# A decoder block on one core: row maxima carried as rows of the score contraction, residual additions on PE, epsilons on ScalarE, and an earlier load of the first weight codes

## The chip, the cores and the metric

The kernel runs on one core of a Trainium2 chip. The metric is the device time in microseconds of one execution, lower is better. The engines are PE (TensorE), DVE (VectorE), ACT (ScalarE), POOL (GpSimd) and SP (SyncE, here only a queue of DMA transfers). PEld is PE's weight load.

## The reference

Input x has 8 batches of 128 tokens and 256 channels. Three blocks follow one another, each on a layer norm of x and added to x:

```python
x = x + attn(layernorm(x), Wq, Wk, Wv, Wo)          # 16 heads of 16, T = 128
x = x + xattn(ctx, ctx, layernorm(x), ssm_kernel, D) # long convolution of k*v products, then times q
x = x + ffn(layernorm(x), gate, up, down)            # 256 -> 2048 -> 256, 4-bit weights with block scales

# attn
scores = einsum('bthd,bshd->bhts', q, k) * tril(ones)   # masked scores are 0, not -inf
out = softmax(scores / T ** 0.5) @ v @ Wo
# xattn, per head of width 8: kv[i,j,l] = k[i,l] * v[j,l]
out = irfft(rfft(kv) * rfft(ssm_kernel)) + kv * D;  out = sum_i out[i,j] * q[i]
# ffn
out = (gelu_tanh(x @ Wg.T) * (x @ Wu.T)) @ Wd.T
```

Since a masked score is 0 and still takes part in the softmax, each row needs the exponential of its negative maximum as well, times the sum of the later values.

## The kernel before

Products that need precision run on PE as three fp16 products of high and low parts (`three`, L927), or in fp32.

Start: x is loaded and normalised, transposed by PE (`transpose_x`), projected to Q and K in two halves of four batches (`project_qk`), with V between and after. Q and K, split in fp16 high and low parts in `nat`, go through a DRAM scratch (L312) and come back packed in `QK` (L322): partitions 0 to 63 hold the even heads, 64 to 127 the odd ones, 64 rows each (high, low and the repeated part). Ten heads of the convolution (`convolve`, L980 to L984) run meanwhile; the other six are spread over the first ticks.

Tick loop: the rest of attention, the second block and the layer norms run as a software pipeline. Every engine walks through the same ticks t, and in each tick through its own hand-written list of steps; `batch(t, T_X)` says which batch a step treats: batch b is treated in tick T_X + 2b. Two ticks pass per batch, the even and the odd one treating half of the heads each. A batch passes, among others:

- tick 0 and 1: `scores(b, p)` on PE into banks 0 and 1, with the causal mask added by products of `identb`/`swapb` with masks (`causal`, L999) and the fp16 contraction of 64 rows (L1016); DVE's `pair_max` (L788) reads the row maxima.
- tick 2, 3: POOL's `guard_max` (L443) copies the maxima with the last row guarded; PE transposes them (L1117), ACT copies them to `mT` (L645) and takes their exponential (L571).
- tick 4, 5: `scores_t` on PE, the transposed scores in banks 2 and 3: masks again (L999), the maxima subtracted by an fp32 product of `sel` with `mT` (L1035), and the contraction (L1039). ACT's `probs` takes the exponential (L579).
- tick 5 to 7: `attend` (L1055), ACT's `pv_out`, token transposes (L1154) and the sum over later values (L1158) on PE, DVE's `normalise`.
- tick 8: transpose of the output (L1133), ACT's copy, projection (L1168), DVE's residual addition (L869) and statistics.
- tick 9, 10: POOL's `rstds` (epsilon L373, power L378, shift L380), ACT's `ln_apply` (L629), query transposes (L1148), ACT's `qx`.
- tick 11 to 15: POOL's `conv_products` (L457, L460), DVE's `sum_slots` (L840), residual and transpose by PE (L1123, L1125), ACT's copy to X (L666), statistics, `rstds`, `ln_apply`, transposes for the FFN (L1141).

Decode: `load_codes(j)` on SP's queue brings step j's codes and scales; `codes_split`, `codes_join` on DVE, `decode_scale` on POOL (L473), `w_hi_step` on ACT (L601) and `w_lo` on DVE (L830) make fp16 high and low weights of them. Steps 0 to 3 do so at the ticks of `DECODE`; steps 0 and 1 use `XN`'s space.

FFN: 32 units, `gate_and_up(u)` (L927, 12 products of 512 columns) and `down(u)` (L1097, 12 of 256 columns). The first eight are placed at `UNIT_TICKS` 22 to 29, the others follow the tick loop. ACT, DVE and POOL each do one operation or two per unit (L618, L608, L848, L481). The order is fixed by the lists and semaphores; nothing is planned at run time. `take(n, sem, count)` makes PE wait for the last reader of bank n.

## Time and profile before

| what | value |
|---|---|
| median of 3 runs | 283.21 us (281.93 to 284.2) |
| profiled execution: its time | 285.32 us |
| profiled execution: its span | 283.6 us |
| mean granted TensorE clock | 0.973 |
| PE busy | 258.4 us (91%) |
| PEld, DVE | 167.5 us (59%), 160.6 us (57%) |
| ACT, POOL | 123.2 us (43%), 157.2 us (55%) |

The span runs from the first to the last instruction of one profiled execution. Busy time of PE is modelled at its ends, so a busy PE need not be at its peak. Busy shares are means over stages that have different limits. A row "start us, us" gives when a group of operations began and how long it took; `x24` is the count.

### The profile page before, as it was taken

To read this page: it belongs to the slowest core of one execution; us is meant where nothing else is said; L and a number is where in the kernel's file an instruction comes from. 1 tells how busy PE (TensorE), PEld (TensorE's weight loads), DVE (VectorE), ACT (ScalarE), POOL (GpSimd) and SP (SyncE) were. 2 spreads that over 40 slices of the span, in tenths; PEclk is the share of its full clock that TensorE was granted. 3 is DMA by queue.
4 is the path that set the end of the run, shared out by engine and by line. 5 is a ranking of instruction groups with operands and counts; after the bars stand their busy time and mean duration, and the time that the engine had idled before them with its cause. 6 is when DMAs were issued, how large, how long until landed. Compare 5 with 4: busy or idle time off the path is not lost.

```text
span 283.6 us, 5339 instructions
## 1 busy us (share of the span) xinstructions
PE 258.4 (91%) x2056; PEld 167.5 (59%) x2056; DVE 160.6 (57%) x264; ACT 123.2 (43%) x257; POOL 157.2 (55%) x193
## 2 busy tenths in 40 slices
PE   0699999997999999996969999999999999999993
PEld 0355766555777777664634566666555666556662
DVE  2879633367775987897576584252635436131124
ACT  2354676553654545644426455323534253442240
POOL 3277264250514788799989897336445563723330
PEclk9999999997999999999579999999999999999998
DMA  6986969707120000003000200000303000000004
GB/s 208 380 296 198 225 203 225 160 4 218 37 82 0 2 2 2 1 3 111 2 0 1 83 30 0 2 0 0 113 0 103 11 0 2 1 0 2 0 0 149
DMA packets 16185, 20.27 MB, mean 71 GB/s; under 512 B 1056, under 2 KB 13856, under 8 KB 16160
## 3 DMA queue, kind: packets, MB, share of 16 engines
q1 hardware_dynamic: 16160, 19.93, 24.4%
q8 instruction: 16, 0.26, 0.4%
q14 instruction: 9, 0.07, 0.1%
HBM read 16.26 MB, written 3.67 MB: 70 GB/s over the span
## 4 chain that ended last, share of the span: by engine, by line
PE 67%; POOL 8%; DMA 7%; DVE 7%; SPq 4%; issue 3%; ACT 2%; DVEq 0%; ACTq 0%; POOLq 0%
PE bank L927 31%; PE bank L1097 14%; PE bank L1035 4%; DMA XN<-in_down_scale 4%; PE bank L999 3%; PE bank L1168 3%; PE bank L1055 3%; POOL w L473 3%; DMA qk_scratch<-pvs 2%; SPq L312 2%; POOL arena L457 2%; POOL arena L460 2%; DMA X<-in_x 1%; DVE arena L741 1%; PE bank L1158 1%
## 5 line engine op out<-in xcount | busy, mean ns | idle before, releaser
L481 POOL TENSOR_TENSOR QK<-QK 128x512 f16<-128x512 f32 x31 | 36.0, 1162 | 56.1 <-ACT QK L608 56.1
L848 DVE SCALAR_TENSOR_TENSOR QK<-bank,QK 128x512 f32<-128x512 f32 x32 | 22.1, 692 | 66.8 <-PE bank L927 66.8
L618 ACT ACTIVATE QK<-bank 128x512 f32<-128x512 f32 x32 | 19.1, 597 | 71.1 <-PE bank L927 71.1
L927 PE MATMUL bank<-xTh,Wa 128*128 128x512 f16 x128 | 40.9, 381 | 0.0
L927 PE MATMUL bank<-xTh,Wb 128*128 128x512 f16 x128 | 40.7, 379 | 0.0
L457 POOL TENSOR_TENSOR arena<-Ys,qx 128x640 f32<-128x640 f32 x16 | 25.1, 1570 | 8.8 <-ACT qx L660 8.8
L579 ACT ACTIVATE PT<-bank 128x1024 f32<-128x1024 f32 x16 | 16.4, 1023 | 27.4 <-PE bank L1039 27.4
L788 DVE TENSOR_REDUCE mx<-bank 128x8 f32<-128x1024 f32 x16 | 19.6, 1222 | 15.1 <-PE bank L1016 15.0
L927 PE MATMUL bank<-xTl,Wa 128*128 128x512 f16 x64 | 24.3, 380 | 0.0
L927 PE MATMUL bank<-xTl,Wb 128*128 128x512 f16 x64 | 24.3, 379 | 0.0
L1097 PE MATMUL bank<-Wa,QK 128*128 128x256 f16 x192 | 23.6, 273 | 0.0
L1097 PE MATMUL bank<-Wb,QK 128*128 128x256 f16 x192 | 23.3, 273 | 0.0
L1035 PE MATMUL bank<-mT,sel 48*128 48x128 f32 x256 | 22.3, 292 | 0.0
L1097 PEld LDWEIGHTS bank<-Wa,QK 128*128 128x128 f16 x192 | 18.7, 98 | 5.7 <-POOL QK L481 0.3
L473 POOL TENSOR_TENSOR w<-arena 128x768 f32<-128x768 f16 x12 | 21.9, 1824 | 0.0
L413 POOL TENSOR_TENSOR arena<-arena 128x320 f32<-128x320 f32 x16 | 14.3, 902 | 13.6 <-PE bank L984 13.6
L1097 PEld LDWEIGHTS bank<-Wb,QK 128*128 128x128 f16 x192 | 18.7, 98 | 5.3
L1035 PEld LDWEIGHTS bank<-mT,sel 48*128 48x128 f32 x256 | 19.6, 190 | 2.6 <-issue 0.3
L927 PEld LDWEIGHTS bank<-xTh,Wa 128*128 128x128 f16 x128 | 12.6, 99 | 13.6 <-issue 0.3
L927 PEld LDWEIGHTS bank<-xTh,Wb 128*128 128x128 f16 x128 | 12.6, 98 | 13.4
L608 ACT ACTIVATE QK<-QK 128x512 f16<-128x512 f32 x32 | 19.9, 621 | 1.0 <-DVE QK L848 1.0
L840 DVE TENSOR_REDUCE R<-arena 128x128 f32<-128x1024 f32 x16 | 19.0, 1209 | 2.1 <-POOL arena L460 2.1
(136 smaller groups left out, 522.1 us busy)
## 6 DMA issues: line engine op xcount, KB each, us to landing
QK<-qk_scratch SPq DMA_DIRECT2D x16, 256.0 KB, 6.0
arena<-in_codes SPq DMA_DIRECT2D x6, 384.0 KB
arena<-in_ker SPq DMA_DIRECT2D x2, 1024.0 KB, 12.5
qk_scratch<-Wa SPq DMA_DIRECT2D x16, 128.0 KB
arena<-in_ctx SPq DMA_DIRECT2D x2, 768.0 KB, 8.1
arena<-in_gu_scale SPq DMA_DIRECT2D x6, 256.0 KB
out<-XN SPq DMA_DIRECT2D x4, 256.0 KB, 2.4
Wb<-in_wqkv SPq DMA_DIRECT2D x3, 256.0 KB, 5.0
```

The lines of the kernel that those rows point to most:

```text
L457: g_.tensor_tensor(view(Z[:, r], [[64, H], [1, NPAIR], [NSLOT, HD]], rows), view(Ys[:, 0, 0], [every, [DIAG, NPAIR], [1, HD]], convolved), ...
L473: g_.tensor_tensor(W32[:, nib, :], view(bits(j).bitcast(F16), [[2, 768]], nib), scales(j), ALU.mult).then_inc(s_w32, 1)
L481: g_.tensor_tensor(il[:, u % IR], val[:, u % VR], ih[:, u % IR], ALU.subtract).then_inc(s_il, 1)
L579: s_.activation(PT[:, 2 * (n % 2):2 * (n % 2) + 2].rearrange("p g h t -> p g (h t)"), psum[:, 2:4, :], ACT.Exp, scale=SCALE).then_inc(s_ex ...
L608: s_.activation(ih[:, u % IR], val[:, u % VR], ACT.Copy).then_inc(s_ih, 1)
L618: s_.activation(val[:, u % VR], bank[2 * (u % 2)][:, :], ACT.Gelu_apprx_tanh, scale=1.0 / W_GAIN).then_inc(s_gel, 1)
L788: v_.tensor_reduce(mx[:, b % 2, 8 * p:8 * p + 8], psum[:, 0:2, :].rearrange("p g (h t) -> p (g h) t", h=4), AX.X, ALU.max).then_inc(s_max, 1)
L840: v_.tensor_reduce(R[:, b % 2, H * half:H * half + H], view(Z[:, b % 2], [[NSLOT, H * HD], [1, NSLOT]], 1024 * half), AX.X, ALU.add).then_ ...
L848: v_.scalar_tensor_tensor(out=val[:, u % VR], in0=bank[2 * (u % 2) + 1][:, :], scalar=UP_SCALE, in1=val[:, u % VR], op0=ALU.mult, op1=ALU. ...
L927: ins = mmul(out, a(c), w(c), start=(n == 0), stop=(n == 3 * len(chunks) - 1))
L1035: mmul(bank[2 + par][:, P * j:P * j + P], view(sel[mrows, 4 * (2 * p + par) + j:4 * (2 * p + par) + j + 1], [[0, P]]), mT[mrows, b % 2, :] ...
L1097: last = mmul(out, a[:, u % IR, t], w[j % RW][:, nib, 512:768], start=((j, nib) == (0, 0) and tt % 2 == 0 and n == 0), stop=((j, nib) == ( ...
```

## The change

- **Row maxima.** `QK` packs 48 rows a half instead of 64 (high, low, and one repeat), and two rows more: on the K side of the transposed pass (`QK[..., 1]`, rows 48 and 49 of each half) the constant -8, on the Q side (`QK[..., 0]`) the row maxima over 8, as an fp16 high and low part. Their product in the contraction subtracts the maximum. DVE makes the parts (`max_pieces`), PE transposes them in fp16, ACT copies them to `mT`, and SP's queue writes them into `QK` by two small DMAs a batch (`max_rows`). The products of `sel` and `mT` go, and so does POOL's `guard_max`.
- **Masks.** `causal` uses two groups of 256 columns a pass instead of one of 512 and one of 256.
- **Residuals.** The first residual, too, is added by an identity product of X into bank 7, and evicted to X by ACT; DVE's addition goes.
- **Epsilons** of the second and third norm are added on ACT (`ln_eps`).
- **Codes.** Step 0's codes are loaded before the second Q/K half goes through the scratch; steps 1 to 3 are issued from ACT's queue.
- **Order.** One convolution head more lies in the ticks; `T_SPLIT`, `T_PROJ`, `T_MIX2` and `T_RT` move by a tick; steps 2 and 3 are decoded at ticks 19 and 23 (before 16 and 22); each engine's list has a new order. PE runs identity products (`keep_busy`) while it waits at the start.

The core of the diff (constants and lists that only swap places are left out):

```diff
-            0, 2, 3, 4, 5, 6, 7, 7, 8, 8, 8, 9, 9, 10, 11, 11, 12, 12, 13, 13, 14, 15, 15)
-        CONV_EARLY = 10
+            0, 1, 3, 4, 5, 6, 7, 7, 8, 9, 8, 9, 9, 10, 11, 12, 12, 12, 13, 13, 14, 15, 15)
+        CONV_EARLY = 9
...
-        DECODE = (1, 5, 16, 22)
+        DECODE = (1, 5, 19, 23)
         DECODE_AHEAD = 7
+        WARM = (18, 4, 6)
...
+            sp.wait_ge(s_const, 3)
             for g in range(2):
-
+                for par in range(2):
+                    sp.dma_start(QK[64 * par + 48:64 * par + 50, g, 1],
+                                 view(minus, [[0, H // 2], [1, HALF]])).then_inc(s_minus, 16)
+            for g in range(2):
+                if g == 1:
+                    load_codes(sp, 0)
...
+                        for part in range(2):
+                            sp.dma_start(scr[g, k, part, :, 8 * m:8 * m + 8],
+                                         nat[g][k][:, m, part, :]).then_inc(s_scr[2 * g + k], 16)
                 for k in range(2):
...
+                        for first, parts, row in ((0, 2, 0), (0, 1, 32)) if k == 0 else ((0, 1, 0), (0, 2, 16)):
...
+            def max_rows(b):
+
+                sp.wait_ge(s_mt, b + 1)
+                for par in range(2):
+                    rows = 64 * par + 48
+                    sp.dma_start(QK[rows:rows + 2, b // 4, 0, :, P * (b % 4):P * (b % 4) + P],
+                                 mT[H * par:H * par + H, b % 2, :]).then_inc(s_rows[b % 2], 16)
+
+            for b in range(B):
+                max_rows(b)
+            for j in range(EARLY, STEPS):
+                load_codes(sp, j)
             for b in range(0, B, 2):
...
-            def guard_max(b):
-
-                r = b % 2
-                pool.wait_ge(s_max, 2 * b + 2)
-                if b >= 2:
-                    pool.wait_ge(s_em, b - 1)
-                    pool.wait_ge(s_mpt, b - 1)
-                g_.tensor_scalar(view(mm[:, r, :], [[64, 2], [1, H]]), view(mx[:, r, :], [[0, 2], [1, H]]),
-                                 guard[:, 0:1], None, ALU.max).then_inc(s_mch, 1)
...
+            def ln_eps(ln, b):
+
+                sc.wait_ge(s_mv[ln], b + 1)
+                s_.activation(veps[:, b:b + 1], mv[:, b, 1:2], ACT.Identity, bias=eps[:, 0:1]).then_inc(s_veps[ln], 1)
...
+                    if j + 1 < EARLY:
+                        load_codes(sc, j + 1)
...
+                for b in batch(t, T_LN2):
+                    sc.wait_ge(s_proj, b + 1)
+                    s_.activation(X[:, b, :], bank[7][:, 0:D], ACT.Copy).then_inc(s_x1, 1)
...
+            def max_pieces(b):
+
+                r = b % 2
+                ve.wait_ge(s_max, 2 * b + 2)
+                if b == 0:
+                    ve.wait_ge(s_const, 7)
+                if b >= 2:
+                    ve.wait_ge(s_em, b - 1)
+                    ve.wait_ge(s_mpt, b - 1)
+                hi = view(mp[:, r], [[16, 2], [4, 2], [1, 4]])
+                lo = view(mp[:, r], [[16, 2], [4, 2], [1, 4]], 8)
+                by_half = [[4, 2], [8, 2], [1, 4]]
+                v_.tensor_scalar(ms[:, r], mx[:, r], guard[:, 0:1], 1.0 / MAX_GAIN, ALU.max, ALU.mult).then_inc(s_ms, 1)
+                v_.tensor_scalar(hi, view(mx[:, r], by_half), guard[:, 0:1], 1.0 / MAX_GAIN,
+                                 ALU.max, ALU.mult).then_inc(s_ms, 1)
+                ve.wait_ge(s_ms, 2 * b + 2)
+                v_.tensor_tensor(lo, view(ms[:, r], by_half), hi, ALU.subtract).then_inc(s_mch, 1)
...
-                    v_.tensor_tensor(X[:, b, :], X[:, b, :], bank[7][:, 0:D], ALU.add).then_inc(s_x1, 1)
...
+            def keep_busy(n):
+
+                for _ in range(n):
+                    mmul(bank[7][:, 0:P], ident[:, :], ident[:, :], start=True, stop=True)
+
...
-            def causal(banks, mask, swapped, full):
+            def causal(banks, transposed):
 
                 half = [slice(0, 64), slice(64, P)]
-                for k in (full, 1 - full):
-                    width = P if k == full else 64
-                    first = 64 if k == 1 and width == 64 else 0
+                for k in range(2):
                     for par in range(2):
                         rows = half[par]
-                        pick, m = (identb, mask) if par == k else (swapb, swapped)
-                        mmul(view(banks[par][:, :], [[P, 4], [1, width]], first), pick[rows, :],
-                             view(m[rows, first:first + width], [[0, 4], [1, width]]),
-                             start=(k == full), stop=False, skip_group_check=True)
+                        if transposed:
+                            pick = (identb if par else swapb) if k == 0 else prevb
+                            m, cut, first = (below, 1, 64) if k == 0 else (below, 0, 0)
+                        else:
+                            pick = (swapb if par else identb) if k == 0 else nextb
+                            m, cut, first = (above, 0, 0) if k == 0 else (above, 1, 64)
+                        mmul(view(banks[par][:, :], [[P, 4], [1, 64]], first), pick[rows, :],
+                             view(m[rows, cut:cut + 64], [[0, 4], [1, 64]]),
+                             start=(k == 0), stop=False, skip_group_check=True)
 
             def scores(b, p):
...
-                        rows = slice(64 * par, 64 * par + 64)
+                        rows = slice(64 * par, 64 * par + 48)
...
                     for par in range(2):
-                        mrows = slice(64 * par, 64 * par + 48)
-                        mmul(bank[2 + par][:, P * j:P * j + P], view(sel[mrows, 4 * (2 * p + par) + j:4 * (2 * p + par) + j + 1], [[0, P]]),
-                             mT[mrows, b % 2, :], start=False, stop=False, skip_group_check=True)
-                    for par in range(2):
-                        rows = slice(64 * par, 64 * par + 64)
+                        rows = slice(64 * par, 64 * par + 50)
...
+                for b in batch(t, T_PROJ):
+                    take(7, s_x1, b + 1)
+                    pe.wait_ge(s_ott, b + 1)
+                    if b == 0:
+                        pe.wait_ge(s_w[3], 16)
+                    mmul(bank[7][:, 0:D], ident[:, :], X[:, b, :], start=True, stop=False)
+                    for c in range(2):
+                        last = mmul(bank[7][:, 0:D], oT[:, b % 2, c, :], wo[:, c, :], start=False, stop=(c == 1))
+                    last.then_inc(s_proj, 1)
```

`load_codes(q, j)` is the same function as before with its queue as an argument. In PE's list of a tick the new order is: projection, plain scores, residual and R transposes, transpose of the maxima, transposed scores, query transposes, FFN transposes, token transposes, output transpose, `attend`, units, convolutions. In ACT's: query copies, `ln_apply` of norm 3, eviction to X of block 2, epsilon of norm 3, output copy, maxima, `probs`, `pv_out`, epsilon of norm 2, units, FFN transposes, decode and its load, `ln_apply` of norm 2, convolutions, eviction to X of block 1.

## Rows read from the trace of the kernel before

**Rows 1.** Windows, all engines: busy us, instructions, granted clock, DMA share, GB/s.

```profile
61.55:72.98 11.43, 9.94 (x153) 7.02 (x154) 7.67 (x9) 4.83 (x6) 2.72 (x4) 0.85 0.48 139
...
81.21:89.66 8.45, 8.45 (x128) 6.32 (x129) 4.96 (x9) 4.13 (x9) 2.19 (x5) 1.00 0.01 2
...
98.10:107.73 9.63, 9.59 (x134) 7.17 (x134) 8.38 (x14) 4.81 (x11) 7.56 (x12) 1.00 0.01 2
107.73:117.19 9.46, 9.12 (x125) 6.95 (x125) 7.12 (x14) 5.09 (x13) 7.54 (x12) 1.00 0.01 2
117.19:126.86 9.67, 8.77 (x112) 6.54 (x111) 9.22 (x16) 5.35 (x12) 9.40 (x9) 1.00 0.01 3
...
137.35:148.46 11.11, 8.31 (x30) 6.47 (x27) 7.80 (x13) 3.61 (x8) 9.48 (x15) 0.65 0.00 0
148.46:277.60 129.14, 128.20 (x787) 77.81 (x786) 55.54 (x75) 49.50 (x84) 69.32 (x61) 1.00 0.06 19
```

**Rows 2.** Chain of work that ended last: start us, us, what.

```profile
12.04 7.26 PE bank L927 x24
...
21.16 0.68 DVE xTl L708
...
46.33 10.01 DMA XN<-in_down_scale
...
268.48 2.59 PE bank L927 x12
271.07 1.31 PE bank L1097 x12
```

**Rows 3.** Timeline of PE, one tick from 81.21: start us, us, what.

```profile
81.21 0.39 PE L999 MATMUL bank<-maskw_t,swapb 64*128 64x512 bf16 x1
...
81.55 0.39 PE L1035 MATMUL bank<-mT,sel 48*128 48x128 f32 x4
...
82.83 0.37 PE L999 MATMUL bank<-maskb,identb 64*128 64x512 bf16 x1
...
83.16 0.39 PE L1016 MATMUL bank<-QK 64*128 64x128 f16 x8
83.47 0.32 PE L1117 MATMUL bank<-ident,mm 128*112 128x128 f32 x1
```

**Rows 4.** Groups by form: count, busy us, mean ns of one, idle before.

```profile
L1123 PE MATMUL bank<-X,ident 128*128 128x256 f32 x16 | 5.3, 418 | 0.0
...
L373 POOL TENSOR_SCALAR veps<-mv 128x1 f32<-128x1 f32 x16 | 4.3, 266 | 8.0 <-DVE mv L697 6.8
...
L869 DVE TENSOR_TENSOR X<-X,bank 128x256 f32<-128x256 f32 x8 | 3.3, 418 | 4.2 <-PE bank L1168 4.2
...
L803 DVE RECIPROCAL rec<-num 128x16 f32<-128x16 f32 x8 | 2.0, 253 | 0.3
...
L571 ACT ACTIVATE em<-mm 128x16 f32<-128x16 f32 x8 | 1.7, 208 | 0.0
```

**Rows 5.** Timeline of POOL, 116 to 139 us.

```profile
116.65 1.56 POOL L457 TENSOR_TENSOR arena<-Ys,qx 128x640 f32<-128x640 f32 x1 [1.38 <-ACT qx L660]
...
124.22 3.77 POOL L473 TENSOR_TENSOR w<-arena 128x768 f32<-128x768 f16 x2
...
138.48 0.27 POOL L380 TENSOR_SCALAR shift<-mv,rstd 128x1 f32<-128x1 f32 x1
```

**Rows 6.** DMA issues: count, KB each, median us to landing.

```profile
QK<-qk_scratch SPq DMA_DIRECT2D x16, 256.0 KB, 6.0
...
out<-XN SPq DMA_DIRECT2D x4, 256.0 KB, 2.4
```

**Rows 7.** Timeline of SP's DMA queue: one load of the codes.

```profile
62.67 0.36 SPq L336 DMA_DIRECT2D XN<-in_codes  x1
63.07 0.61 SPq L338 DMA_DIRECT2D XN<-in_gu_scale  x1
63.73 0.59 SPq L341 DMA_DIRECT2D XN<-in_down_scale  x1
```

More of the change, by code:

```diff
@@ L314, in _ @@
                 for k in range(2):
[L315 removed]
+                    sp.wait_ge(s_scr[2 * g + k], 64)
                     for par in range(2):
[L317 to L323 removed]
@@ L387, in _ @@
                     g_.memset(vaug[:, :, :, DH:DH + 1], 1.0).then_inc(s_const, 1)
-            for m, sign in ((maskb, 1), (mask_t, -1)):
+            half = [slice(0, 64), slice(64, P)]
+            for m, keep, base in ((above, ALU.is_ge, 0), (below, ALU.is_ge, -1)):
+                sign = 1 if m is above else -1
                 own(g_.memset(m[:, :], 0.0))
-                own(g_.affine_select(out=m[:, :], in_=m[:, :], compare_op=ALU.is_ge, fill=NEG, base=0,
-                                     pattern=[[-sign, P]], channel_multiplier=sign))
-            for m, sign in ((maskw, 1), (maskw_t, -1)):
-                own(g_.memset(m[:, :], 0.0))
-                for half, base in ((slice(0, 64), 64), (slice(64, P), 0)):
-                    own(g_.affine_select(out=m[half, :], in_=m[half, :], compare_op=ALU.is_ge, fill=NEG,
-                                         base=sign * base, pattern=[[-sign, P]], channel_multiplier=sign))
+                for rows in half:
+                    own(g_.affine_select(out=m[rows, :], in_=m[rows, :], compare_op=keep, fill=NEG, base=base,
+                                         pattern=[[-sign, 65]], channel_multiplier=sign))
             own(g_.memset(swapb[:, :], 0.0))
@@ L662, in _ @@
                                   ACT.Copy).then_inc(s_qx, 1)
+                for b in batch(t, T_APPLY3):
+                    ln_apply(2, b)
                 for b in batch(t, T_LN3):
@@ L855, in _ @@
                     w_lo(j)
-                for b, p in pair_of_groups(t, T_SCORES):
-                    pair_max(b, p)
+                for b in batch(t, T_SUM2):
+                    sum_slots(b, 1)
+                for h in conv_heads(t + 1):
+                    if h >= KVR:
+                        products(h)
+                for b in batch(t, T_LN2):
+                    ve.wait_ge(s_x1, b + 1)
+                    ln_stats(1, b)
+                for j in early_decode(t, 0):
+                    codes_split(j)
+                    codes_join(j)
+                for b in batch(t, T_SPLIT):
+                    max_pieces(b)
                 for b in batch(t, T_LN3):
@@ L1113, in _ @@
                     scores(b, p)
-                for b in batch(t, T_MPT):
-                    take(7, s_mt, b + 1)
-                    pe.wait_ge(s_mch, b + 1)
-                    t_.transpose(bank[7][0:112, 0:P], mm[:, b % 2, :], ident[:, :]).then_inc(s_mpt, 1)
                 for b in batch(t, T_RT):
@@ L1142, in _ @@
                     last.then_inc(s_yt, 1)
-                for b in batch(t, T_QT):
-                    take(6, s_qx, 2 * b + 2)
-                    pe.wait_ge(s_xn[1], b + 1)
-                    for c in range(2):
-                        last = t_.transpose(bank[6][:, P * c:P * c + P], XN[:, b, P * c:P * c + P], ident[:, :])
-                    last.then_inc(s_qt, 1)
                 for b in batch(t, T_TOK):
```

257 lines of the change are left out of this document (130 added, 127 removed).

## The prediction

> **What bounds the kernel now.** I read the windows first, cut at the places where the attention projection of a batch (L1168) ends or the tick loop enters a new stretch, then the chain of waits, then the order of PE's work inside one tick.
>
> PE is the busy engine nearly everywhere, but for three different reasons. From 148.46 on it is full: 128.20 us busy out of 129.14 [rows 1]. In the chain this is one pattern repeated: 2.59 us of L927, then 1.31 us of L1097, 3.90 us a unit [rows 2]; 32 units are 124.8 us, and the change leaves them alone. So the end is the time at which unit 0 starts, plus about 129 us, plus the 6 us behind it. Between 61.55 and 117.19 PE is busy as well (8.45 of 8.45; 9.59 of 9.63), but with attention work that the change cuts [rows 1]. From 117 to 148 PE has gaps (8.77 of 9.67, then 8.31 of 11.11 at a granted clock of 0.65), while POOL is busy for 9.40 and 9.48 us: POOL sets the pace there, with DVE close to it (9.22) where a decode step falls in [rows 1]. A saving on PE passes through whole in the first stretch only as far as DVE (8.38 of 9.63) lets it, and in the last only if POOL's queue also starts earlier.
>
> **Part 1: row maxima as two rows of the contraction.** One tick's PE order is in [rows 3]. The transposed pass takes 0.34 us of masks (81.21 to 81.55) and 1.28 us of body (81.55 to 82.83), where L1035 adds the maxima in fp32 beside the fp16 products. The plain pass has masks of 0.33 and a body of only 0.31 (83.16 to 83.47). The new transposed body is of that form, 50 rows deep: it saves 0.97 a pass, 1.94 a batch. The masks shrink from 512 + 256 columns to 256 + 256, two thirds: 0.11 for each of four mask groups, 0.44 a batch. The transpose of the maxima shrinks too; I give it 0.1. Against this stands one more identity product per batch for the residual; L1123 is the same product, 5.3 us for eight batches, 0.66 each with modelled ends [rows 4]; I take 0.5. Net 2.0 us a batch, 16 us of PE work.
>
> What is added elsewhere: DVE loses the residual addition (0.42) and gets three operations on 16 or fewer elements a batch; the nearest row is the reciprocal of 16 elements, 0.25 [rows 4]. So DVE goes up by 0.3 a batch. POOL loses its maximum operation and two epsilons (0.27 each, about 0.3 with the gap); ScalarE gets them, nearest row L571 with 0.21 [rows 4], and gets the eviction of X.
>
> The maxima now travel by DMA: ScalarE's copy, two issues on SP, a landing, then PE's transposed pass. The trace has no small transfer on a quiet queue. The nearest rows are 2.4 us for the output and 6.0 for the packed Q/K rows, both 256 KB [rows 6]; an issue costs 0.36 to 0.61 [rows 7]. I take the output's value: 0.3 + 2 x 0.5 + 2.4 = 3.7 us. Behind the transpose PE has, until the pass that needs the rows, a transposed pass (0.55), the attention products and token transposes (about 1.5) and a plain pass (0.55): 2.6 us, 3.0 where the later transposes join. So PE waits about 1 us a batch while PE is the bound, and nothing where DVE or POOL is. Behind that wait on PE lie the query transposes, the attention products and the projection; ScalarE's exponentials wait for it. The Trainium skill, "DMA: Bandwidth & Descriptors" (section "Anatomy of one DMA"), puts the fixed part of a transfer at about 2.0 us; by that the wait would be 0.6, and the sum some 2 us lower over the early batches. No row here shows so small a transfer.
>
> **Part 2: the start.** PE does its first 24 projection products in 7.26 us [rows 2]; 24 at the late rate (2.59 / 12 = 0.216) are 5.2. The added identity products fill the idle start, so that these may run at the higher clock: 2.1 us. But the second projection waits for DVE's split of x, which ends at 21.84 [rows 2] after DVE operations that hang on POOL and on x, not on PE. I pass on 0.8 us (ends 0 and 2). Moving one convolution head behind tick 0 shifts work, and saves none.
>
> **Part 3: the first codes.** The 10.01 us transfer of the first codes stands in the chain [rows 2]; it ends at 56.34, and decode, ScalarE's conversion and DVE's rest follow. The window 61.55 to 72.98 is 11.43 us long for 9.94 busy at clock 0.85 [rows 1]: 1.5 us idle and about 1.7 us of slow clock. Loading the first codes ahead of the second Q/K half takes this chain off the ticks; the second half is needed four batches later. But the other three early loads move to ScalarE, in order with its exponentials: 0.36 + 0.61 + 0.59, 1.6 us each with their gaps [rows 7]. Two fall in early ticks beside a 1.5 us weight conversion. I let these and the first DMA round trip eat what the early codes give. Ticks 4 to 8 have five transposed and five plain passes: 5 x (0.97 + 0.22) = 5.9 us; I take 5 (ends 2 and 8).
>
> **Part 4: the middle.** Before, four batches from 81.21 to 117.19 take 8.45 (twice), 9.63 and 9.46 [rows 1]. The first two come to 8.45 - 2.0 + the wait = 6.9 and 7.3. In the last two PE would need 7.6, but DVE then needs 8.38 + 0.3 = 8.7: DVE takes over. Sum 31.6 against 36.0: 4.4 us. The reordered ticks keep the dependences in step; I cost the order itself at nothing, since each wait it adds (residual before statistics, maxima before row copies) has a pass of PE between. Without that cover each costs the 0.4 to 0.6 of one eviction.
>
> **Part 5: up to unit 0.** Before, POOL runs without a gap worth naming from the first product of batch 3 (116.65) to the end of the shift of batch 3 (138.75), 22.1 us [rows 5]; unit 0 follows 9.7 later, at 148.46. Two things leave this chain: the decode of step 2 (3.77, [rows 5]), which moves from tick 16 to 19, so that POOL's part comes behind that point; and five epsilons, 1.6. Left are 16.7 us. It starts 0.8 + 5 + 4.4 earlier, at about 107, and ends at 124. The 9.7 behind it had the projection of the last batch in it, which now comes after unit 0 (about 2 at the low clock), and a clock of 0.65 (some 2.5); I take 5. Unit 0 starts at 129 instead of 148.46: 19.5 us earlier.
>
> **Part 6: the tail.** After unit 0 the 129.14 us stay; added are the last projection with its identity (1.5), query transposes, and idle time of PE, since vector and POOL work is now squeezed beside the first eight units: 1.5. So 3 us go back.
>
> Sum: 283.6 - 19.5 + 3 = **267.1 us of span**. The profiled execution had a time of 285.32 and a span of 283.6; the median of the runs is 283.21, about the span. I predict **267 us**.
>
> **The rivals.** (a) The saving turns into waiting. With 2 us less work in each batch PE idles more, and idle PE lost clock: 11.11 us for 8.31 busy at 0.65 [rows 1]. If the three batches before unit 0 still take 10 us each, and an early tick falls back as well, unit 0 starts near 137 and the span is about 275. For it speaks that the chain crosses POOL, ScalarE's queue and DMA more often; against it, that PE's work stays near 80% of a batch.
> (b) The full PE saving and more: DVE's and POOL's work packs tighter than I think, the early codes save their 3 us whole, and the DMA is covered. Then the start gives 2, ticks 4 to 8 give 8, the middle 7, Part 5 its own 9.3, and the tail takes 1: the span is 258 to 260. DVE's 8.7 speaks against.
> (c) Slower: the round trip through SP. If the landing is like the packed rows' 6.0 [rows 6], the trip is 7.3 and PE waits 4.7 in each batch; a batch takes 7.6 + 4.7 = 12.3 against a mean of 9.6 between 81.21 and 148.46. Eight batches lose 22, less the 9 of the start, the early passes and the codes: about 296. It turns from gain to loss where the landing passes some 4 us. For it: the rows of this queue. Against it: those stood in a crowd of transfers; DMA share is 0.01 from 81.21 on [rows 1].
> (d) Nothing comes through, since ScalarE's new loads, evictions and epsilons hold the exponentials: 283. ScalarE is busy only 4.13 to 5.35 us a batch [rows 1], which speaks against.
>
> **How the numbers follow.** Forecast 0.55 (262 to 272), (a) 0.22, (b) 0.12, (c) 0.05, (d) 0.06. Leaving out most of (c), (d) and the edges of (b) gives 257 to 278. One per cent is 2.8 us, about what a measurement here can tell from no change. Faster 0.89, within 0.05, slower 0.06.
>
> **What would show it.** Right: no L1035 group; the transposed pass as short as the plain one; first projection products 0.216 us apart; the first unit near 129; DVE above 90% of a batch where scores and slot sums overlap; unit length still 3.90. Wrong: transposed passes released by DMA after more than 1 us of idle PE; a granted clock under 0.8 over whole batches; ScalarE's exponentials queued behind DMA issues; gaps between the first eight units above 3 us in all, which would be a tail that gives the gain back.

## Result and the profile after

| | before | changed |
|---|---|---|
| median | 282.72 us (281.55 to 284.35, 14 runs) | 280.38 us (278.18 to 282.77, 14 runs) |
| ratio, 95% interval | | 0.990 (0.987 to 0.993) |
| span of the profiled execution | 283.6 us | 278.3 us |
| PE, DVE busy | 258.4, 160.6 us | 250.9, 162.5 us |
| ACT, POOL busy | 123.2, 157.2 us | 129.9, 149.3 us |

The change makes the kernel 1.0% faster; I had forecast 5.7% (267 us) and a range that ended 2.4 us below the measured time. PE's busy time fell by 7.5 us on balance, with some 9 us of identity products at the start (L959) in it, so that about 16 us of work did go, as forecast. The trace before is of an execution of 285.32 us, 2.6 above the median of its kernel; that after is of one of 280.03, close to its median. So the two spans differ by 5.3 us and the medians by 2.3, and some 3 us of what the traces show between the two kernels belong to that one execution.

Windows of the changed kernel, with the columns of [rows 1]. The cuts lie where the projection of a batch starts with its residual product (0.5 us ahead of its first product with the weights, which is the time that the text gives for a projection); the last window starts with the seventh unit. Unit 0 starts at 138.96.

```profile
59.28:76.72 17.44, 11.26 (x196) 7.53 (x195) 14.38 (x21) 8.11 (x16) 3.63 (x2) 0.90 0.26 87
76.72:84.64 7.92, 7.28 (x103) 5.10 (x100) 6.35 (x12) 5.45 (x12) 1.67 (x3) 1.00 0.01 3
92.12:101.48 9.36, 8.08 (x103) 5.53 (x104) 8.93 (x17) 5.46 (x14) 5.99 (x7) 1.00 0.01 3
101.48:111.12 9.64, 7.84 (x94) 5.39 (x94) 8.93 (x18) 6.22 (x16) 7.00 (x9) 1.00 0.02 4
119.84:130.80 10.96, 8.15 (x72) 5.70 (x69) 8.36 (x16) 5.66 (x13) 7.72 (x10) 0.81 0.00 0
130.80:143.23 12.43, 9.58 (x40) 6.07 (x37) 8.00 (x13) 7.39 (x14) 12.23 (x11) 0.78 0.42 126
169.46:272.30 102.84, 102.84 (x639) 62.28 (x637) 38.44 (x51) 36.80 (x62) 45.11 (x36) 1.00 0.05 16
```

In the batches at 92 and 101 PE has about 8 us of work, 1.3 to 1.5 less than before [rows 1], but a batch still takes 9.36 and 9.64, about what it took. DVE is busy 8.93 where I had 8.7, and that is too little to explain it: what counts is the order in which the two alternate. The chain of waits of the changed kernel, over the end of one batch:

```profile
96.91 0.47 PE bank L1213 x2
97.41 0.45 DVE tail L842
97.88 0.45 DVE num L846
98.36 0.26 DVE rec L849
98.64 1.73 DVE o_sb L851
100.51 0.41 PE bank L1219 x2
100.92 0.56 PE bank L1108 x16
101.48 0.67 PE bank L1163 x2
```

PE's sum over later values (L1213), then DVE's four operations of `normalise`, then PE's transpose of the output (L1219), attention products and the next projection: PE and DVE take turns. The last operation of `normalise` is the long one. The timeline of the changed kernel shows what runs beside it, and four more rows from the early ticks:

```profile
62.20 0.28 PE L1056 MATMUL bank<-below,swapb 64*128 64x256 bf16 x1 [2.30 <-DMA QK<-mT]
67.14 3.63 POOL L492 TENSOR_TENSOR w<-xTh,XN 128x768 f32<-128x768 f16 x2 [10.14 <-DVE xTh L871]
67.38 1.66 DVE L836 TENSOR_TENSOR mp<-ms,mp 128x16 f16<-128x16 f32 x1
70.23 0.28 PE L1056 MATMUL bank<-above,identb 64*128 64x256 bf16 x1 [2.55 <-DVE mx L816]
...
98.52 1.57 POOL L476 TENSOR_TENSOR arena<-Ys,qx 128x640 f32<-128x640 f32 x1
98.64 1.72 DVE L851 TENSOR_TENSOR o_sb<-num,rec 128x256 f32<-128x256 f32 x1
100.03 1.21 POOL L479 TENSOR_TENSOR arena<-Ys,qx 128x384 f32<-128x384 f32 x1
```

`o_sb` started 0.12 us behind a POOL product and ended 0.3 us after it. The difference of the maxima (L836), an operation on 16 elements, took 1.66 us beside POOL's decode, whose two products take 1.8 each. Over the kernel, from the groups by form of the changed kernel:

```profile
L851 DVE TENSOR_TENSOR o_sb<-num,rec 128x256 f32<-128x256 f32 x8 | 8.1, 1015 | 0.3
L836 DVE TENSOR_TENSOR mp<-ms,mp 128x16 f16<-128x16 f32 x8 | 4.4, 547 | 0.3
```

My theory (A): such DVE operations, with two inputs in SBUF, stand until POOL's operation is over, and the shorter PE passes no longer cover them. The rivals were the round trip of the row maxima by DMA (B), the half clock after PE's waits (C), and the epsilons moved to ScalarE (D), since POOL waited 25.6 us for these in all.

### The profile page after: what moved, and what is told of

The parts are those of the page before. It is cut to its first block, busy times and chain, and to the rows that moved or that the text cites. A ratio compares the mean times of both kernels' runs of the same rounds, so it can differ in the third digit from the quotient of the medians.

```text
span 278.3 us, 5004 instructions
## 1 busy us (share of the span) xinstructions
PE 250.9 (90%) x1872; PEld 161.9 (58%) x1872; DVE 162.5 (58%) x280; ACT 129.9 (47%) x281; POOL 149.3 (54%) x172
## 4 chain that ended last, share of the span: by engine, by line
PE 56%; DVE 5%; POOL 4%; issue 3%; ACT 2%; DVEq 0%; POOLq 0%; ACTq 0%
PE bank L980 30%; PE bank L1150 15%; PE bank L1165 2%; PE bank L1163 2%; POOL w L492 1%; PE bank L1177 1%; DVE o_sb L851 1%; POOL arena L476 1%; PE bank L1179 1%; PE bank L1108 1%; DVE XN L946 1%; ACT XN L651 1%; POOL rstd L403 1%; POOL arena L479 1%; PE bank L1203 1%
## 5 line engine op out<-in xcount | busy, mean ns | idle before, releaser
L980 PE MATMUL bank<-xTh,Wa 128*128 128x512 f16 x128 | 41.9, 389 | 0.0
L980 PE MATMUL bank<-xTl,Wa 128*128 128x512 f16 x64 | 25.0, 391 | 0.0
L403 POOL TENSOR_TENSOR rstd<-veps,nhalf 128x1 f32<-128x1 f32 x16 | 9.6, 597 | 25.6 <-ACT veps L643 25.6
L725 DVE BATCH_NORM_STATS2 stats<-X 128x6 f32<-128x256 f32 x24 | 10.0, 417 | 19.0 <-ACT X L712 10.6
L446 POOL TENSOR_TENSOR arena<-arena 128x320 f32<-128x320 f32 x16 | 13.7, 865 | 12.0 <-PE bank L1038 12.0
L479 POOL TENSOR_TENSOR arena<-Ys,qx 128x384 f32<-128x384 f32 x16 | 20.1, 1256 | 0.0
```

Of the source, the lines that this page charges most:

```text
L446: g_.tensor_tensor(view(KV[:, h % KVR, m, :], [[40, B], [8, NPAIR], [1, HD]]), view(a, [[12 * H, B], [0, NPAIR], [1, HD]]), view(a, [[12 * ...
L479: g_.tensor_tensor(view(Z[:, r], [[64, H], [1, 3], [NSLOT, HD]], rows + NPAIR), view(Ys[:, 0, 0], [every, [DIAG - 1, 3], [1, HD]], convolv ...
L980: ins = mmul(out, a(c), w(c), start=(n == 0), stop=(n == 3 * len(chunks) - 1))
```

## The experiments

Times are medians; each ratio is to the kernel before, run beside it. "Numerator in PSUM" is the kernel of the first experiment, "pieces first" that of the tenth.

**1. Numerator in PSUM** (changed kernel; `normalise` writes its sum back into its own bank, so that its last operation has one input in SBUF):

```diff
-                v_.tensor_tensor(num[:, :, :], tail[:, :, :], view(bank[4 + b % 2][:, :], [[32, H], [1, DH + 1]]),
-                                 ALU.add)
+                num_p = view(bank[4 + b % 2][:, :], [[32, H], [1, DH + 1]])
+                v_.tensor_tensor(num_p, tail[:, :, :], num_p, ALU.add)
...
-                        pe.wait_ge(s_och, 4 * (b - 2) + 2)
+                        pe.wait_ge(s_och, 4 * (b - 2) + 4)
```

> The sum of normalise is written back into its PSUM bank, so that the last multiplication of normalise (1.37 to 1.72 us from batch 1 on in the changed kernel, 0.42 when POOL rests) has no second large SBUF input. Theory A, that a loop of PE and DVE through normalise sets the pace and that this multiplication waits there for POOL's product: it falls to about 0.45 in every batch, some 1.0 us less in each of seven batches, 5 to 7 us in all: 274 to 276, ratio 0.97 to 0.975. Theory B, that DMA round trips and the slow clock set the pace: the multiplication gets short, but the time stays within 1 us of 280.4 (ratio 0.99). Theory C, that POOL's queue sets the pace: no change either.

275.01 us, ratio 0.973 (0.970 to 0.976). The group by form of this kernel:

```profile
L851 DVE TENSOR_TENSOR o_sb<-bank,rec 128x256 f32<-128x256 f32 x8 | 3.4, 424 | 0.3
```

The same operation on the same data: 424 ns each time instead of 1015 in the mean. In five of the eight batches a POOL product began before it and ended after it. The batches take 7.41, 7.42, 8.65 and 8.66 us instead of 7.42, 7.99, 9.36 and 9.64. One extra wait of `attend` costs nothing that can be seen. A stands for `normalise`.

**2. No rows by DMA** (no `max_rows`; the Q rows 48 and 49 are filled with the constant once, so that the maxima aren't subtracted in the transposed pass).

```diff
-            for b in range(B):
-                max_rows(b)
...
-                    if p == 0:
-                        pe.wait_ge(s_rows[b % 2], 32 * (b // 2 + 1))
```

> Leaves out the copies of the row maxima: the two rows of Q hold a constant, so no maximum is subtracted (the output is not the reference's). PE's waits for these transfers are 2.30, 0.82 and about 0.2 to 0.45 in four later batches, some 4.3 us in the trace. Theory B (the round trip is the main loss): 4 to 6 us faster, 275 to 276, ratio 0.975. Theory A: the first 3 us are partly taken over by DVE, which is busy 14.4 of 17.4 us there, and the later ones by the normalise chain: 0 to 2.5 us faster, 278 to 280.

280.78 us, ratio 0.991 (0.987 to 0.995), as the changed kernel. B falls for this kernel: even the wait of 2.30 us at 62.20 isn't what holds the stage. Without the rows PE reaches the next wait earlier and stands there for DVE's maxima instead, 4.00 us where the changed kernel had 2.55 (70.23 above). Timeline of this kernel:

```profile
69.77 0.39 PE L1053 MATMUL bank<-above,identb 64*128 64x256 bf16 x1 [4.00 <-DVE mx L813]
```

What the rows cost once the collision ahead of them is gone, this run can't show (see 11).

**3. Epsilons on POOL**, as before the change.

```diff
+                    own(g_.tensor_scalar(veps[:, n0:n0 + n], mv[:, n0:n0 + n, 1], EPS, None, ALU.add))
...
-                for b in batch(t, T_RSTD2):
-                    ln_eps(1, b)
```

> The epsilons of norms 2 and 3 go back to POOL, as before the change. POOL waited 25.6 us in all for them in the changed kernel. If the hand-over between the engines is on the path (theory D): 2 to 4 us faster, 276 to 278. If only slack is behind this wait (theory A): 0 to 2 us slower, 280 to 282, since POOL gets 0.3 us more per norm.

282.41 us, ratio 0.998 (0.994 to 1.002): 2 us slower, so D falls, as far as it concerns the epsilons. The trace shows that it isn't 2 us of epsilons: POOL's later products now miss `normalise` (0.42 us in seven batches of eight) and meet the pieces of the maxima instead. In three batches L830, the pieces' second operation, takes 1.61 us instead of 0.23 and L833, their difference, 0.93 instead of 0.17, and these batches are 9.18 to 11.28 us long. The collision moved, and cost more in its new place.

**4. Cover by order**: in PE's list the plain scores stand ahead of the projection, and `attend` ahead of the output transpose.

> Only PE's order changes: attend before the output transpose, plain scores before the projection, so that 0.56 us of other work lies behind the wait for normalise and 0.55 behind the copy of its transpose. Theory A: the loop gets 0.5 us shorter in each of some seven batches, 3 to 4 us faster, 276.5 to 277.5, ratio 0.98. Theories B, C and D: unchanged, within 1 us of 280.4.

280.64 us, ratio 0.993 (0.989 to 0.996): a miss. The timeline of this kernel:

```profile
100.67 1.54 DVE L851 TENSOR_TENSOR o_sb<-num,rec 128x256 f32<-128x256 f32 x1
```

The operation is as long as it was. From the third projection to the seventh this kernel takes 36.5 us instead of 39.2, so the cover gives there about what I expected, but it has lost 2.5 us by the third projection, and unit 0 comes at 140.05 instead of 138.96. I take it that the chain goes on through DVE's own queue (pair maxima, then scores, projection and statistics); no run takes that apart.

**5. Numerator in PSUM, in the kernel before.**

> The kernel before, with the numerator kept in PSUM in the same way. My theory: the slow last operation of the normalise (1.4 us beside a POOL product, 0.42 without) costs time only where the shorter PE passes no longer cover it, so it is a cost that the change uncovered. Then the kernel before gains little by this edit: 281 to 283. Rival: the collision was on the path before as well, and the edit is worth its 5 to 7 us to either kernel: 276 to 278; then the comparison of change and no change stays at 1% with the collision gone too.

282.19 us, ratio 0.998 (0.995 to 1.001). The source line's durations, least, median and most, before (first line) and with the edit (second):

```profile
L805 DVE TENSOR_TENSOR o_sb<-num,rec x8: 424/426/1243, 77.7 to 144.1; 128x256 f32<-128x256 f32 x8
```

```profile
L805 DVE TENSOR_TENSOR o_sb<-bank,rec x8: 424/424/424, 77.3 to 141.9; 128x256 f32<-128x256 f32 x8
```

Before, the operation met a POOL product in three batches (1.20, 0.89 and 1.24 us), and the medians say that it was covered there, or nearly: 0.7 us between them, within the interval. The change moved the two engines' work so that they meet in most batches, and took away the cover. So the change is worth 7.2 us where both kernels have this edit (282.19 to 275.01), and 2.3 where neither has.

**6. No identity products at the start** (`WARM = (0, 0, 0)`).

> The changed kernel without the identity products that fill PE's waits at the start. If they gave the whole of the 1.75 us by which the first convolution head starts earlier, the time is 282 and the first 24 projection products take 7.2 us instead of 5.2. Rival: the start waits for x and DVE, not for the clock: 280.4 as the changed kernel, with the head at 28.7 again.

281.96 us, ratio 0.997 (0.993 to 1.000), 1.6 us slower than with them. Timeline, PE, the changed kernel (first) and this one (second):

```profile
11.90 0.39 PE L980 MATMUL bank<-xTh,w 128*128 128x512 f16 x1
12.13 0.38 PE L980 MATMUL bank<-xTl,w 128*128 128x512 f16 x1
...
28.66 0.70 PE L1034 MATMUL bank<-arena 128*128 128x320 f32 x2
```

```profile
12.26 0.61 PE L980 MATMUL bank<-xTh,w 128*128 128x512 f16 x1 [1.42 <-DVE xTl L738]
12.66 0.63 PE L980 MATMUL bank<-xTl,w 128*128 128x512 f16 x1
...
31.34 0.70 PE L1034 MATMUL bank<-arena 128*128 128x320 f32 x2
```

The first products start some 0.22 us apart instead of 0.43 (2.4 and 1.2 GHz), after PE had been busy instead of idle; the convolution starts 2.7 us earlier. Here the clock is on the path.

**7. Decode steps 2 and 3 two ticks later** (numerator in PSUM; `DECODE = (1, 5, 21, 25)`).

> Changed kernel with the numerator in PSUM (275.0), and decode steps 2 and 3 two ticks later (21 and 25), so that POOL's 3.6 us of step 2 leave the chain that ends at unit 0. If POOL sets the start of unit 0, it comes at 132 instead of 135.7 and the time is 272 to 273, with some of it lost again between the units. Rival: these units need the weights and wait for the decode, or ACT and PE set the start: 275 or more.

283.56 us, ratio 1.002 (0.998 to 1.005): a miss. Unit 0 comes at 133.66, 2 us earlier, and then PE stands for the weights of step 3:

```profile
170.47 0.61 PE L980 MATMUL bank<-xTh,Wb 128*128 128x512 f16 x1 [6.17 <-DVE Wb L876]
```

**8. Decode step 1 two ticks later** (numerator in PSUM; `DECODE = (1, 7, 19, 23)`).

> Changed kernel with the numerator in PSUM (275.0), and decode step 1 two ticks later (7). In the traces DVE's difference of the maxima took 1.66 us instead of 0.18 beside POOL's decode, behind four code operations (2.6 us), and PE stood for 2.8 us and came back at half clock. If it is the place of the decode that costs this, the first projection (78.6 us) comes 2 to 3 us earlier: 272 to 273. Rival: the decode costs as much wherever it lies, since DVE is the bound of these ticks: 275.

278.85 us, ratio 0.984 (0.978 to 0.990): a miss. The collision moved with the step (L836 1.66 us at 73.56), now with `normalise` behind it, and PE stood 3.92 us for `o_sb`. (The trace is of the longest of the four executions, 280.83.)

**9. Step 2 alone one tick later** (numerator in PSUM; `DECODE = (1, 5, 20, 23)`).

> Changed kernel with the numerator in PSUM (275.0), and decode step 2 alone one tick later (20), step 3 as it was (23). With both two ticks later unit 0 came 2 us earlier, but PE stood 6.2 us for the rest of step 3's weights at 164. If that wait was the whole of the loss, step 2 alone gives 274 to 275. Rival: the late step 2 disturbs the units as much as it helps unit 0: 276 or more.

278.32 us, ratio 0.982 (0.977 to 0.987): the rival. The chain of waits of this kernel shows why: the load of step 3's codes is issued behind the conversion of step 2, and step 3's code operations wait for it.

```profile
137.50 0.36 ACTq L301
...
138.54 7.51 DMA arena<-in_down_scale
...
146.07 1.29 DVE arena L859
```

**10. Pieces first** (numerator in PSUM; DVE's list has `max_pieces` ahead of the codes):

```diff
+                for b in batch(t, T_SPLIT):
+                    max_pieces(b)
                 for j in early_decode(t, 0):
                     codes_split(j)
                     codes_join(j)
-                for b in batch(t, T_SPLIT):
-                    max_pieces(b)
```

> Changed kernel with the numerator in PSUM (275.0), and in DVE's list the pieces of the maxima ahead of the code operations of step 1. The 1.66 us difference then runs before POOL's decode and takes 0.18, and the scores that PE waited for 2.8 us come 1.5 us earlier. If DVE's chain in tick 5 sets the stage, the first projection comes 1.5 to 2.5 us earlier: 273. Rival: the decode step comes later by as much and pays it back at its conversion and rest: 275.

273.69 us, ratio 0.963 (0.959 to 0.967), the fastest whole kernel. Timeline of this kernel:

```profile
65.39 0.17 DVE L836 TENSOR_TENSOR mp<-ms,mp 128x16 f16<-128x16 f32 x1
...
68.17 3.58 POOL L492 TENSOR_TENSOR w<-xTh,XN 128x768 f32<-128x768 f16 x2 [10.46 <-DVE xTh L871]
```

The operation is over before POOL's decode begins. The first projection starts at 75.30 instead of 78.63. (Kernels that are alike up to that point had it at 77.35 to 78.63 without the edit and at 74.82 to 76.07 with it, so about 2 us are the edit's; the medians differ by 1.3 us, the ratios by 1%.) What is left of PE's idle time in this stage is mostly the wait for the first rows of the maxima, in the timeline of PE:

```profile
62.61 0.28 PE L1056 MATMUL bank<-below,swapb 64*128 64x256 bf16 x1 [2.92 <-DMA QK<-mT]
```

**11. Narrow codes of step 1** (numerator in PSUM; DVE's code operations and POOL's products of step 1 treat 96 of 768 columns).

> Changed kernel with the numerator in PSUM (275.0); the code operations on DVE and the scale products on POOL of step 1 treat 96 of 768 columns, so that the weights of step 1 are not the reference's; all else runs as before. It takes some 2.3 us from DVE and 3.1 from POOL in ticks 5 and 6, and the collision with the difference of the maxima. If this work beside the attention ticks ate the gain that I forecast for ticks 4 to 8, the first projection comes at 75 to 76 instead of 78.6 and the time is 272. Rival: the stage is held by its own chain (maxima, rows, exponentials), and the time stays within 1 us of 275.

274.41 us, ratio 0.968 (0.965 to 0.971). Taking most of the step away gives no more than putting three small operations ahead of it, though it takes the collision away too (L837, the same difference, 0.24 us at 66.18). The trace has the reason:

```profile
74.36 0.28 PE L1059 MATMUL bank<-below,swapb 64*128 64x256 bf16 x1 [2.69 <-DMA QK<-mT]
```

With the step short, ScalarE issues the load of step 2's codes from 69.63 on, while SP issues the rows of the maxima from 69.39 on; the second transfer of the rows lands 4.3 us behind its issue, and the chain of waits of this kernel goes through it (4.29 us at 70.03) as well as through the two ahead of it (3.64 at 59.07 and 1.75 at 65.26). So with the collision gone the round trip (B) is on the path, up to 2.7 us of it here. No run takes the rows away in the kernel with the pieces first, where PE stands for them 2.92 us; what that wait costs there stays open.

**12. Clock kept up** (numerator in PSUM; identity products into a bank that PE owns, ahead of six waits).

```diff
+                    stay_busy({5: 8, 6: 10, 7: 3}.get(b, 0), 6)
```

> Changed kernel with the numerator in PSUM (275.0), with identity products on PE before six waits: 9 ahead of the first transposed pass, 12 ahead of the plain pass of tick 6, and 8, 10 and 3 ahead of the query transposes of batches 5 to 7. They cost nothing where PE waits anyway. If the half clock after these waits costs time (5 us at half clock after 70.8, 3 us in unit 0), the first projection comes 1 to 2 us earlier and unit 0 is followed sooner: 272 to 273. Rival: PE isn't the bound in the slow stretches, and the time stays at 275.

275.98 us, ratio 0.973 (0.968 to 0.977), as without. Windows of two stretches, without (first) and with:

```profile
59.30:78.00 18.70, 13.69 (x196) 8.63 (x194) 14.34 (x22) 8.38 (x17) 3.63 (x2) 0.73 0.25 84
118.00:135.00 17.00, 11.57 (x88) 8.59 (x88) 12.80 (x26) 10.23 (x22) 15.62 (x18) 0.90 0.15 43
```

```profile
59.30:78.00 18.70, 15.69 (x241) 12.07 (x240) 15.98 (x23) 9.01 (x17) 3.64 (x2) 1.00 0.26 85
118.00:135.00 17.00, 13.78 (x124) 11.21 (x122) 12.64 (x26) 9.08 (x20) 14.19 (x15) 1.00 0.11 31
```

The granted clock is 1.00 in both stretches, and nothing is won. The first projection comes at 78.01, inside the 77.35 to 78.63 of the kernels without these products, so in the first stretch C falls. In the second the test isn't clean: eight of the identity products started at 124.32, when the norm that the query transposes wait for had already ended (124.20), and held these transposes until 126.20, 16.0 us after the fifth projection instead of 14.2.

**13. Clock kept up ahead of unit 0** (pieces first; 3 and 5 identity products).

> Numerator in PSUM and pieces first (273.7), with 3 and 5 identity products ahead of the query transposes of batches 5 and 6 only. In the trace without them unit 0 takes 4.15 us instead of 2.59, and the projection ahead of it 1.71 instead of 0.86, at half clock and in the chain. If that counts here, the time is 272 to 272.5. Rival: as with the many identity products on the version before, the clock rises and the time stays at 273.7, since DVE and POOL set the pace.

274.86 us, ratio 0.970 (0.964 to 0.976), no gain, though in the kernel without them unit 0 took 4.15 us in the chain. Here the products ended ahead of the wait's end. The trace is of an execution of 272.59 us, the fastest of four that reach to 276.07; from the fifth projection to unit 0 it took 25.3 us (25.6 without), and from unit 0 to the end 137.7 (139.2). So the shorter end is of one execution, and the medians show no gain.

**14. Narrow step 2** (pieces first; step 2 treats 96 of 768 columns on DVE and POOL).

> Numerator in PSUM and pieces first (273.7, the best so far), and the codes and scale products of step 2 treat 96 of 768 columns (its weights are not the reference's). My Part 5 took POOL's 3.6 us for step 2 out of the chain that ends at unit 0, yet in every trace it runs before unit 0. If this is the missing term, unit 0 comes 3 to 4 us earlier than 133.1 and the time is 270 to 271. Rival: ScalarE's conversion and loads (1.5 us and three issues, unchanged here) or PE at half clock set unit 0, and the time stays within 1 us.

269.04 us, ratio 0.950 (0.945 to 0.955). Timeline of POOL, pieces first (first fence) and this kernel (second):

```profile
124.11 3.58 POOL L492 TENSOR_TENSOR w<-arena 128x768 f32<-128x768 f16 x2
```

```profile
122.96 0.73 POOL L493 TENSOR_TENSOR w<-arena 128x96 f32<-128x96 f16 x2
```

Unit 0 starts at 129.84 instead of 133.08. This decode is 4.6 us of the time, 2.8 of them between the fifth projection and unit 0. The edit shortens DVE's code operations as well as POOL's products, so the share of each isn't shown; in the changed kernel's chain of waits POOL's part stands between the statistics and unit 0:

```profile
130.64 3.59 POOL w L492 x2
```

**15. Steps 2 and 3 at ticks 16 and 22**, as before the change (pieces first).

> Numerator in PSUM and pieces first (273.7), with decode steps 2 and 3 at ticks 16 and 22 as before the change. If the later place is worth something, this is slower: DVE is at 8.65 of 8.66 us in those batches and takes 2.6 us more there, 275 to 276. Rival: the place is as good as another (POOL's 3.6 us come before unit 0 in both), 273.7.

273.55 us, ratio 0.966 (0.962 to 0.970), the same as at 19 and 23. The new places are worth nothing. (The 8.65 and 8.66 us of my expectation are the lengths of these two batches; DVE is busy for 8.27 and 7.19 of them.)

**16. Pieces first alone** (changed kernel, numerator in SBUF).

> The changed kernel with the pieces of the maxima ahead of the codes alone, the numerator still in SBUF (280.4 without). If the two collisions cost independently, the gain is the 2 to 2.6 us that it gave with the numerator in PSUM: 278. Rival: behind the slow normalise the earlier ticks 4 to 8 are lost again: 280.

279.14 us, ratio 0.982 (0.974 to 0.990). The first projection comes at 75.33, but the middle batches are again 9.36 and 9.63 long. The median is 1.2 us below 280.4, and the interval leaves open how much is lost behind the slow `normalise`.

**17, 18. Step 2 at tick 10 and at tick 12** (pieces first).

> Numerator in PSUM and pieces first (273.7), with decode step 2 at tick 10 instead of 19. In that trace DVE idles for 2.3 us (82 to 84.2) and POOL for 1.9 (84.4 to 86.3) in tick 10, where the step needs 2.6 and 3.6. If the 3.6 us of POOL ahead of unit 0 are the missing term, most of the 4.6 us that narrowing the step gave come without leaving work out, less 1 to 2 us in the early batches: 270 to 271.5. Rival: the early batches lose as much as unit 0 gains: 273.7 or more.

> The same with decode step 2 at tick 12, where slot sums already fill DVE (8.65 us of 8.66 from batch 2 on). Between the two: 271 to 273. Rival: as for tick 10, or worse since DVE is full there: 274.

276.83 us, ratio 0.979 (0.976 to 0.981), and 277.02, ratio 0.980 (0.976 to 0.984): both misses. At tick 10 the timeline has:

```profile
88.81 1.80 POOL L492 TENSOR_TENSOR w<-arena 128x768 f32<-128x768 f16 x1
89.89 0.76 DVE L832 TENSOR_SCALAR ms<-mx,guard 128x16 f32<-128x16 f32 x1
90.56 1.61 DVE L833 TENSOR_SCALAR mp<-mx,guard 128x16 f16<-128x16 f32 x1
90.58 1.56 POOL L476 TENSOR_TENSOR arena<-Ys,qx 128x640 f32<-128x640 f32 x1
92.09 1.00 POOL L479 TENSOR_TENSOR arena<-Ys,qx 128x384 f32<-128x384 f32 x1
92.20 0.92 DVE L836 TENSOR_TENSOR mp<-ms,mp 128x16 f16<-128x16 f32 x1
```

Each of DVE's three small operations, 0.6 us together elsewhere, ends with the POOL operation beside it, 3.3 us in all; that batch takes 13.3 us instead of 7.4. Of these 5.9 us the collision is thus 2.6, and the code operations on DVE (2.6 us) are about as much. From the fifth projection to the eighth it is 5.8 us faster than with the step at tick 19 (24.5 against 30.3), so the gain was there, and the three batches ahead lost 7.6. Idle time of DVE and POOL, from which I had taken the place, didn't show this.

## Why the prediction was wrong

The terms, from the first projection (before: 80.18) over the fifth (116.15) and unit 0 (148.46) to the end (283.6):

| stretch | before | forecast | changed | numerator in PSUM | pieces first | narrow step 2 |
|---|---|---|---|---|---|---|
| start to first projection | 80.18 | -5.8 | 77.22 (-3.0) | 78.63 | 75.30 (-4.9) | 74.82 |
| four batches | 35.97 | -4.4 | 34.41 (-1.6) | 32.14 (-3.8) | 32.15 | 32.15 |
| fifth projection to unit 0 | 32.31 | -9.3 | 27.33 (-5.0) | 24.88 | 25.63 | 22.87 (-9.4) |
| unit 0 to the end | 135.14 | +3.0 | 139.34 (+4.2) | 137.65 | 139.22 | 137.66 (+2.5) |

With the two collisions and the decode gone, the span is 267.5 us against 267.1 forecast, and each stretch is within 0.6. So most of the sum was read right, and three terms weren't. That the agreement is so close is in part luck: my forecast moved step 2's decode behind unit 0, while this kernel leaves most of it out, and the column "before" is the long execution of 285.32 us. (With the numerator in PSUM the kernel before, in an execution of 282.82, took 28.69 us from the fifth projection to unit 0, 3.6 less, so that the third row's differences may hold up to that much of chance.) I also took the span for the time; in every run here the time is 1.7 to 1.8 us above it.

**The order costed at nothing (Part 4).** This is the step that failed. I wrote that each wait "has a pass of PE between" and that without this cover an eviction's 0.4 to 0.6 would be the price. `normalise` wasn't among the waits that I named. The cover was gone for it, and the operation wasn't 0.42 but up to 1.72 long. The trace had it: before, L805 took 1.20 us in one batch and 0.42 in the next, and I had averaged DVE's time by windows. It is worth 5.4 us (280.4 to 275.0). Once the collision was gone the two later batches took 8.65 and 8.66, as long as the 8.7 for which I had DVE "take over", but not by that reason. Windows of the kernel with the numerator in PSUM:

```profile
93.46:102.11 8.65, 7.85 (x104) 5.55 (x103) 8.26 (x17) 5.35 (x14) 5.92 (x7) 1.00 0.01 3
102.11:110.77 8.66, 7.74 (x95) 5.39 (x94) 7.19 (x16) 6.11 (x16) 6.55 (x8) 1.00 0.02 5
```

DVE is full in neither, and the chain of waits over these 17.3 us has DVE in it for 1.6; the rest goes through PE, ScalarE and POOL in turn. That the length fits is luck in part.

**Ticks 4 to 8 (Part 3).** The forecast was 5 us, of which some 1.2 came (3.0 less the start's 1.75), and 3.1 with the pieces first. I had DVE's new operations at 0.25 us each from their size; L836 took 1.66 in the tick of step 1. The loads on ScalarE's queue and the first round trip, which I had blamed in advance, cost nothing behind the collision (2), but they show once it is gone: a wait of 2.92 us for the first rows (10), and one of 2.69 beside the load of step 2's codes (11). In the quiet ticks of the changed kernel the round trip was shorter than I had it: from PE's transpose at 95.61 to the pass at 98.67 it took 3.1 us instead of 3.7, and PE waited at most 0.45 us a batch instead of 1. The 2.0 us of the Trainium skill that I had named beside it ("DMA: Bandwidth & Descriptors", section "Anatomy of one DMA") are a figure for transfers that GpSimd issues; on SP's queue a transfer with no load beside it landed 1.75 us behind its issue (65.26 in 11).

**The decode that stayed (Part 5).** I took the 3.77 us of step 2 out of the chain, "so that POOL's part comes behind that point". Tick 19 still lies ahead of unit 0 at tick 22, and its 3.58 us stand in POOL's queue there. Narrowing the step gave 4.6 us; moving it anywhere else gave none, since each place either collides (ticks 10 and 12), is equal (16) or starves the units (20 and 21).

**What held.** The PE saving (transposed pass as short as the plain one, 0.56 us), the unit length of 3.90 us (102.84 us busy of 102.84 at the end), and roughly the tail's 3 us (4.2 in the changed kernel, 2.5 with step 2 narrow), of which one wait at 168.27 for a slot sum behind POOL (1.58 us) is the largest piece. The start gave twice my 0.8: 1.75 in the trace, 1.6 by experiment 6. Rival (a), 275 and 0.22, had the right shape, saving turned into waiting, but its mechanism, idle PE that loses clock, isn't it: clock restored gave nothing that the medians show (12, 13). (c) was refuted by the time itself and by experiment 2, (d) by 3 for the epsilons; ScalarE's evictions weren't tested. I had put 0.05 on "within 1%", and the result fell on that edge.

## What to carry to other kernels

When a change shortens the bound engine's work, price what then becomes the hand-over: look for an operation of the other engine whose duration varies from batch to batch, and ask what runs beside it, since a mean by group or a window hides it. A tensor operation of DVE with both inputs in SBUF, begun beside a long POOL operation, cost here what was left of the POOL operation, 1.66 us for 16 elements; keep one input in PSUM, or put it ahead of what starts POOL, and look where the collision goes when you move anything, since it can land on the next small operation (3, 8, 17). A run that takes one cost away while a longer wait stands behind it shows nothing about that cost (2 against 11). Whether a step leaves a chain is read from the order of its engine's queue, not from its tick number.

## What the runs showed of the hardware

- A DVE operation with two SBUF inputs was held by a POOL operation that had begun before it: 16 elements a partition took 1.66 us instead of 0.17, 256 took 1.72 instead of 0.42, each ending with the POOL operation or up to 0.3 us after it. With one input in PSUM the same operation took 424 ns eight times out of eight, five of them beside a POOL product. The Trainium skill, "SBUF — State Buffer" (section "Who interferes with whom"), says that such an instruction contends with a POOL instruction that reads SBUF, for a port pair that one of them holds for the whole instruction; by that rule the trace agrees.
- Scalar operations with one tensor input were held as well (L833 1.61 us instead of 0.23; the first code operation, 768 elements, 1.2 instead of 0.53), and reductions of 1024 elements from SBUF never (1.20 to 1.22 us in all runs). The same section lets operations with one SBUF input contend only in DVE's two-port modes; no run here shows which mode they ran in.
- Two transfers of 4 KB each, issued beside a load of codes, let PE go on 4.5 us after the first issue (57.74 to 62.20); in experiment 11 the second of them took 3.64 and 4.29 us beside such loads and 1.75 without, and there the chain of waits went through all three.
- The clock rose and fell with what PE had done before, but only at the start was this on the path: 1.6 us there, and nothing that could be seen for a window that went from 0.73 to 1.00.
